# Block-local attention: a group's keys fetched ahead of its queries, with the keys' wait set to their last reader

## The chip, the cores and the metric

The kernel runs on one core of one Trainium2 chip. Its time is device microseconds (us) for one execution, from the first to the last instruction plus what the launch adds around them; the number compared is the median of several executions. One execution was also recorded by the hardware profiler, and all rows below are from it. The engines are PE (TensorE matmul), PEld (its weight loads), DVE (VectorE), ACT (ScalarE), POOL (GpSimd) and SP (SyncE, which in this kernel only issues DMAs, in one queue and in program order).

## The reference, cut to what matters

The program is a two-layer network on x of 8 x 1024 x 128 floats (batch B = 8, T = 1024 tokens, C = 128 channels). The change touches only the first attention:

```python
q, k, v = (layernorm(x) @ W.T split into 16 heads of 8)    # for Wq, Wk, Wv
# tokens in blocks of 64; a block's queries see the block before and their own
scores = q_block @ concat(k_before, k_block).T / sqrt(8)   # 64 x 128 per head
scores = where((j > i) & (j <= i + 64) & not_before_the_first, scores, -1e30)
out    = softmax(scores) @ concat(v_before, v_block)
x      = x + out @ Wo.T
```

Ahead of it stands a gated low-rank expert layer with its normalisation; behind it stand the same layer once more, a quantised product, a latent attention with 8 heads, and the quantised product again.

## The kernel before, in words

The window attention (the stage that the change touches) works in 16 groups: group hb is half hb % 2 of batch hb // 2, so 512 tokens, all 16 heads. A group is 8 steps (HB = 8), one per block of 64 tokens; step n = 8 hb + m. The whole stage is one software pipeline over n, written out by hand. In step n TensorE does, in program order:

- at m = 0 the transposition of the previous group's row maxima (`pe_window_maxima(hb - 1)`, L1013), and only then
- the scores of step n with queries as rows (`pe_window_scores`, its mask product is L1085, its scores L1090). Scores of step n wait for VectorE's maxima of step n - 1, and at m = 0 for the group's queries and keys to have landed (`moved(hb, 0)` and `moved(hb, 1)`, L1079 to L1081);
- the scores of step n - 10 with keys as rows (`pe_window_key_rows`, L1035 and L1042), which count up `key_rows` at 2n + r; at m = 0 they wait for the maxima that SP has moved (L1026);
- the weighing with the values of step n - 12 and later (L1061), the turning back (L1070), and "parts" that a planner placed in two spare banks: among them the projection of group hb's queries and keys ("once", L842), due ten steps ahead of the group.

Queries and keys need a layout that one product can't give: each value split in a high and a low part, and replicated over partitions. So each group goes through memory. ScalarE copies the product's high part into the tile `once` and VectorE the rest (L876, L905); SP writes `once` to `rows_mem` in HBM (`sync_spread`, 8 DMAs for the queries, i = 0, then 8 for the keys, i = 1), and brings it back (`sync_gather`): the queries with 4 DMAs of 256 KB in pieces of 256 bytes (L952), the keys with one DMA of 1 MB in pieces of 2 KB (L948). A gather waits until all of its own writes have landed (`bounced[i]`, L946), and for its place in on-chip memory to be free: the queries' three buffers by L943, the keys' two batches by L945. Both are waits on `key_rows`.

SP's program for the stage (L2135 to L2142) is, for each hb in order: spread queries, spread keys, gather queries, gather keys, and then `sync_move_maxima(hb - 1)` (L971, 4 small DMAs), which waits for the maxima of group hb - 1 to be copied by ScalarE, that is for TensorE to stand at the start of group hb. The next iteration's spread also waits until the gathers of this one have landed (L926). So between the start of group hb - 1 on TensorE and the start of group hb, SP moves the maxima of group hb - 2, spreads group hb and gathers group hb.

Of the kernel before, what the change touches and what calls it, by code (L numbers as in the profile page):

```python
# [27 lines left out]
HB = NB // 2  # L28
# [269 lines left out]
def build_program(nc, x_in, w128, w_mla, w_out_window, w33, w1, consts, out):  # L298
    ctx = ExitStack()
    with ctx:  # L300
# [8 lines left out]
        def signal(name):  # L309
            counts.append(Count(new_sem(name)))  # L310
            return counts[-1]
# [499 lines left out]
        key_rows, exps = signal("window_scores_by_key"), signal("window_exponentials")  # L811
# [110 lines left out]
        def sync_spread(e, hb, i):  # L922


            if hb:
                e.wait_ge(*moved(hb - 1, i))  # L926
            e.wait_ge(*part_act.at(("once", hb, i)))
            e.wait_ge(*part_dve.at(("once", hb, i)))
            for h in range(4):
                rows = slice(h * REP * D0, (h + 1) * REP * D0)  # L930
                into = rows_mem[i, h].rearrange(("(x y) d q c -> y (d q) x c", "(x y) d q c -> x (d q) y c")[i], x=2)
                e.dma_start(into[0], once[rows, i].bitcast(F32)).then_inc(bounced[i], 16)
                e.dma_start(into[1, :, 0], once[rows, i, 0].bitcast(F32)).then_inc(bounced[i], 16)

        def sync_gather(e, hb, i):

            b, half = divmod(hb, 2)
            e.wait_ge(*last_rows_stored)
            if i == 0:
                if hb < QUERY_BUFS:  # L940
                    e.wait_ge(*set_pool.at(("slots", hb)))
                else:
                    e.wait_ge(*key_rows.at(2 * HB * (hb - QUERY_BUFS + 1) - 1))  # L943
            elif b >= 2:
                e.wait_ge(*key_rows.at(2 * HB * (2 * (b - 2) + 2) - 1))  # L945
            e.wait_ge(bounced[i], 128 * (hb + 1))  # L946
            if i:
                e.dma_start(keys[:, b % 2, :, W + half * HALF:W + (half + 1) * HALF].bitcast(F32),  # L948
                            rows_mem[1].rearrange("h p d q c -> (h p d) q c")).then_inc(k_moved[hb % 2], 16)
                return  # L950
            for h in range(4):
                e.dma_start(queries[h * REP * D0:(h + 1) * REP * D0, hb % QUERY_BUFS, :, :, h % 2, :].bitcast(F32).rearrange(  # L952
                    "p q n w -> p (q n) w"),
                    rows_mem[0, h].rearrange("p d q (n w) -> (p d) (q n) w", w=W)).then_inc(q_moved[hb % 2], 16)

        def sync_last_rows(e):


            e.wait_ge(*set_pool.at("last rows"))
            for i in range(2):  # L960
                for h in range(4):
                    e.dma_start(rows_mem[i, h, REP - 1].rearrange("d q c -> (d q) c"),
                                last_rows[:, i, :]).then_inc(last_rows_stored[0], 16)

        def sync_move_maxima(e, hb):

            e.wait_ge(*mx_copied.at(hb))
            for r in range(2):
                for s in range(2):
                    row = (2 * r + s) * REP * D0 + (REP - 1) * D0  # L970
                    e.dma_start(queries[row:row + 1, hb % QUERY_BUFS, :, :, s, :].bitcast(F32).rearrange(  # L971
                        "o q m w -> o (q m) w"),
                        mx_rows[r * QUADS * HB:(r + 1) * QUADS * HB, hb % 2, s * W:(s + 1) * W].bitcast(F32)).then_inc(
                        mx_moved[hb % 2], 16)
# [884 lines left out]
        def sync_move_shift(e, u, i):  # L1859

            e.wait_ge(*shift_steps.at((u, i, 2)))
            queries_free(e, u)
            for t in range(4 * i, 4 * i + 4):
                e.dma_start(q_low[KR:KR + 1, u % Q_BUFS, t * P:(t + 1) * P].bitcast(F32).rearrange(
                    "o (p t) -> o p t", t=1), shift_cols[:, i, t % 4:t % 4 + 1].bitcast(F32)).then_inc(
                    shift_moved[u % Q_BUFS][i], 16)
# [89 lines left out]
        def sync_move_head(e, u):  # L1956

            b, h = divmod(u, NH)
            rows = slice(h % 4 * DC, (h % 4 + 1) * DC)
            if h == 0 and b >= 2:  # L1960
                e.wait_ge(*projected.at((b - 2, 1)))
            e.wait_ge(*o_ready.at(u))
            for q in range(4):
                e.dma_start(o_allT[rows, b % 2, h // 4, q * QUARTER:(q + 1) * QUARTER],
                            o_norm[q * DC:(q + 1) * DC, u % 2, :]).then_inc(o_moved[u % 2], 16)
# [156 lines left out]
        def sync_store(e, b):  # L2122
            e.wait_ge(*x_dve.at(("d", b)))
            e.dma_start(outr[:, b], x[:, b * NT:(b + 1) * NT, :]).then_inc(s_out, 16)

        def sync(e):
            e.dma_start(first_rows[:, :], x_in[:, 0, :]).then_inc(first_landed[0], 16)
            e.dma_start(x[:, 0:NT, :], xr[:, 0]).then_inc(x_landed[0][0], 16)
            e.dma_start(cst[:, :], consts).then_inc(const_landed[0], 16)
            for dst, src in ((Wt, w128), (Wo, w_out_window), (Wt33, w33), (Wt1, w1)):  # L2130
                e.dma_start(dst[:, :], src).then_inc(weights_landed[0], 16)
            for b in range(1, B):
                e.dma_start(x[:, b * NT:(b + 1) * NT, :], xr[:, b]).then_inc(x_landed[b][0], 16)
            sync_last_rows(e)
            for hb in range(2 * B + 1):  # L2135
                if hb < 2 * B:
                    for i in range(2):
                        sync_spread(e, hb, i)
                    for i in range(2):
                        sync_gather(e, hb, i)  # L2140
                if hb:
                    sync_move_maxima(e, hb - 1)  # L2142
            e.wait_ge(*gate_steps.at(("a", "y")))
            for b in range(B):
                e.wait_ge(*x_dve.at(("w out", 2 * b)))
                e.dma_start(first_rows[b:b + 1, :], x[0:1, b * NT, :]).then_inc(first_landed[1], 16)
            e.wait_ge(*x_dve.at(("w", B - 1)))
            e.wait_ge(*weighed.at(units // 4 - 1))
            e.dma_start(Wm[:, :], w_mla).then_inc(mla_landed[0], 16)
            for u in range(B * NH + 2):  # L2150
                if u < B * NH:
                    for i in range(2):
                        sync_move_shift(e, u, i)
                if u >= 2:
                    sync_move_head(e, u - 2)
                b, h = divmod(u, NH)
                if h == 3 and 2 <= b < B:
                    sync_store(e, b - 2)
            sync_store(e, B - 2)
            for half in range(2):  # L2160
                e.wait_ge(*x_dve.at(("d", B - 1, half)))
                ts = slice(half * NT // 2, (half + 1) * NT // 2)
                e.dma_start(outr[:, B - 1, ts], x[:, (B - 1) * NT + half * NT // 2:(B - 1) * NT + (half + 1) * NT // 2, :]
                            ).then_inc(s_out, 16)
            e.wait_ge(s_out, 16 * (B + 1))
# [9 lines left out]
        @block.sync  # L2175
        def _(eng):
            sync(eng)
# [81 lines left out]
```

## Time and profile before

| | us |
|---|---|
| median of 3 runs (lowest to highest) | 1809.43 (1809.35 to 1809.67) |
| the profiled execution, its own time | 1814.3 |
| its span, first to last instruction | 1812.5 |
| PE busy in the span | 1670.4 (92%) |
| DVE busy | 1393.8 (77%) |
| ACT busy | 1137.5 (63%) |
| POOL busy | 1177.3 (65%) |
| window attention, first to last scores of a step (L1085) | 73.6 to 456.2 |
| mean granted TensorE clock, share of full speed | 0.967 |

The page divides the span into 40 slices of 45 us. The DMA engines are busy in the first ten of them (0.4 to 0.6 of their time, 116 to 164 GB/s) and nearly idle from slice 12 on; those ten are the loads, the first expert layer and the window attention. A share is a mean over the 16 DMA engines; packets in flight at the same time on one engine count each, so a short stretch can show slightly more than 1.

### The profile page before, as it was taken

What the parts mean: (1) busy time and instruction counts of PE and PEld (TensorE: products, weight loads), DVE (VectorE), ACT (ScalarE), POOL (GpSimd) and SP (SyncE); (2) the same over time, 40 slices, a digit from 0 to 9 for tenths busy, and PEclk for the clock granted to TensorE, in tenths of its full rate; (3) what the DMA queues carried; (4) which work ended last, traced back from release to release, by engine and by line L of the source; (5) the groups of instructions that cost most, each with busy time, mean ns of one, the idle gap of its engine ahead of it and who ended that gap; (6) DMA issues with size and microseconds to landing.
All of it is one profiled execution on the core that took longest, in us unless ns stands there. A gap on an engine that the chain in (4) does not pass through costs nothing.

```text
span 1812.5 us, 39662 instructions
## 1 busy us (share of the span) xinstructions
PE 1670.4 (92%) x15057; PEld 1223.0 (67%) x15057; DVE 1393.8 (77%) x2976; ACT 1137.5 (63%) x2222; POOL 1177.3 (65%) x909
## 2 busy tenths in 40 slices
PE   4679999999877899999999999999999999999995
PEld 4557777777766567666766766766676677677674
DVE  5557777766597888878888888888887888888862
ACT  5447777777676466666666666666656666665662
POOL 4300111000066498898898988989889898898892
PEclk9889999999887899999999999999999999999997
DMA  4556666654000000000000000001001000100101
GB/s 123 136 140 156 162 156 159 164 136 116 29 1 1 1 10 8 10 8 10 7 13 16 10 8 19 11 7 22 7 10 19 8 10 7 22 7 10 19 10 30
DMA packets 198677, 81.47 MB, mean 45 GB/s; under 512 B 152553, under 2 KB 177493, under 8 KB 198357
## 3 DMA queue, kind: packets, MB, share of 16 engines
q1 hardware_dynamic: 198484, 78.93, 19.5%
q8 instruction: 119, 1.95, 0.5%
q14 instruction: 74, 0.60, 0.1%
HBM read 39.79 MB, written 29.88 MB: 38 GB/s over the span
## 4 chain that ended last, share of the span: by engine, by line
PE 54%; DVE 11%; POOL 2%; issue 1%; ACT 1%; DMA 0%; SPq 0%; POOLq 0%; ACTq 0%
PE pair L1825 12%; PE pair L1878 11%; PE pair L1882 11%; PE pair L1936 10%; DVE amax L1833 4%; PE pair L1929 4%; PE pair L1650 2%; DVE o_inv L1946 1%; PE pair L1641 1%; DVE stats L485 1%; POOL w_mix L1907 1%; PE pair L1664 1%; DVE q_low L1754 1%; DVE cq L1765 1%; DVE key_hl L1768 1%
## 5 line engine op out<-in xcount | busy, mean ns | idle before, releaser
L1893 ACT ACTIVATE prob<-pair 128x512 f32<-128x512 f32 x1024 | 604.4, 597 | 422.2 <-PE pair L1882 359.6
L1833 DVE TENSOR_REDUCE amax<-pair 128x1 f32<-128x512 f32 x1024 | 670.3, 682 | 133.9 <-PE pair L1825 131.8
L1825 PE MATMUL pair<-key_hl,q_hi 128*128 128x512 f32 x1024 | 437.8, 430 | 11.2 <-DVE amax L1833 7.1
L1878 PE MATMUL pair<-q_hi,key_hl 128*128 128x512 f32 x1024 | 405.2, 396 | 2.6 <-ACT prob L1893 2.6
L1882 PE MATMUL pair<-q_low,key_h 65*128 65x512 f32 x1024 | 406.0, 396 | 0.0
L1907 POOL TENSOR_TENSOR w_mix<-w_mix,prob 128x1024 f32<-128x1024 f32 x160 | 382.3, 2389 | 25.2 <-ACT prob L1893 8.5
L1907 POOL TENSOR_TENSOR Wm<-Wm,prob 128x1024 f32<-128x1024 f32 x155 | 369.6, 2384 | 20.8 <-ACT prob L1893 4.1
L520 POOL TENSOR_SCALAR veps<-mv 128x8 f32<-128x8 f32 x47 | 11.4, 243 | 452.6 <-DVE mv L493 451.2
L1825 PEld LDWEIGHTS pair<-key_hl,q_hi 128*128 128x128 f32 x1024 | 196.1, 192 | 115.9 <-issue 51.0
L1936 PE MATMUL pair<-prob,values 128*32 128x256 f32 x4096 | 247.2, 382 | 0.0
L1186 DVE TENSOR_REDUCE mx_neg<-pair 128x4 f32<-128x512 f32 x256 | 164.9, 687 | 94.8 <-PE pair L1090 94.1
L1878 PEld LDWEIGHTS pair<-q_hi,key_hl 128*128 128x128 f32 x1024 | 195.5, 191 | 44.3 <-ACT prob L1893 9.4
L1882 PEld LDWEIGHTS pair<-q_low,key_h 65*128 65x128 f32 x1024 | 192.5, 188 | 44.6
L1936 PEld LDWEIGHTS pair<-prob,values 128*32 128x32 f32 x4096 | 127.5, 110 | 100.9 <-issue 25.0
L1136 ACT ACTIVATE yT<-pair 128x512 f32<-128x512 f32 x256 | 138.6, 593 | 72.3 <-PE pair L1042 70.3
L1946 DVE RECIPROCAL o_inv<-pair 128x256 f32<-128x256 f32 x64 | 112.5, 1758 | 59.8 <-PE pair L1929 59.8
L542 ACT ACTIVATE y<-x,mean_neg,rstd 128x128 f32<-128x128 f32 x336 | 137.7, 485 | 19.0 <-POOL mean_neg L528 18.9
L1090 PE MATMUL pair<-keys,queries 64*128 64x128 f32 x1024 | 100.5, 317 | 0.0
L1042 PE MATMUL pair<-queries,keys 64*128 64x128 f32 x1024 | 97.0, 309 | 0.0
L1702 ACT ACTIVATE q_hi<-pair 128x512 fp32r<-128x512 f32 x128 | 75.7, 591 | 20.0 <-PE pair L1641 20.0
L1754 DVE TENSOR_TENSOR q_low<-pair,q_hi 64x512 fp32r<-64x512 f32 x128 | 86.3, 675 | 2.2 <-ACT q_hi L1702 2.2
L1090 PEld LDWEIGHTS pair<-keys,queries 64*128 64x128 f32 x1024 | 82.7, 199 | 3.7
(209 smaller groups left out, 2232.8 us busy)
## 6 DMA issues: line engine op xcount, KB each, us to landing
rows_mem<-once SPq DMA_DIRECT2D x128, 128.0 KB, 2.0
queries<-rows_mem SPq DMA_DIRECT2D x64, 256.0 KB, 4.5
keys<-rows_mem SPq DMA_DIRECT2D x16, 1024.0 KB, 7.1
rows_mem<-once SPq DMA_DIRECT2D x128, 64.0 KB, 1.9
q_low<-shift_cols SPq DMA_DIRECT2D x512, 0.5 KB, 2.0
yT<-o_norm SPq DMA_DIRECT2D x256, 32.0 KB, 1.9
x<-x_dram SPq DMA_DIRECT2D x8, 512.0 KB, 7.3
out_dram<-x SPq DMA_DIRECT2D x7, 512.0 KB, 3.4
```

The lines of the kernel that those rows point to most:

```text
L542: ins = e.activation(y_of(stage, b)[:, t, :], x[:, b * NT + t, :], ACT.Identity, bias=mean_neg[:, k, t:t + 1], scale=rstd[:, k, t:t + 1])
L1090: ins = e.matmul(bank(S_BANKS[r])[:, q * P:(q + 1) * P], queries[rows, hb % QUERY_BUFS, q, m].rearrange("p s w -> p (s w)"), keys[rows, b ...
L1136: e.activation(pT[:, u % P_TURNED].rearrange("p q k -> p (q k)"), key_row_bank(*divmod(u, 2)), ACT.Exp).then_inc(*exps.up(u))
L1186: e.tensor_reduce(mx_neg[:, hb % 2, r, :, m], bank(S_BANKS[r]).rearrange("p (q k) -> p q k", q=QUADS), AX_X, ALU.max, negate=True).then_in ...
L1825: e.matmul(row_bank(("row", r, i)), q_hi[:, k, t * P:(t + 1) * P], key_hl[:, b % 2, i * HALF:(i + 1) * HALF], start=True, stop=True, skip_ ...
L1833: e.tensor_reduce(amax1[:, u % 2, t, i:i + 1], row_bank(("row", r, i)), AX_X, ALU.max).then_inc(*row_maxed.up((r, i)))
L1878: e.matmul(bank(j), key_hl[:, b % 2, ks], q_hi[:, k, sl], start=True, stop=False, skip_group_check=True)
L1882: e.matmul(bank(j), key_h1[:, b % 2, ks], q_low[:, k, sl], start=False, stop=True, skip_group_check=True).then_inc(*key_scored.up((g, half)))
L1893: e.activation(prob1[:, g % P_BUFS, half * HALF:(half + 1) * HALF], bank(K_BANKS[(2 * g + half) % 3]), ACT.Exp, scale=SCALE1).then_inc(*ke ...
L1907: e.tensor_tensor(into, into, p, ALU.add).then_inc(*summed_keys.up(g))
L1936: ins = e.matmul(bank(PVB)[q * DC:(q + 1) * DC, 0:QUARTER], values[:, b % 2, t, :], prob1[:, g % P_BUFS, q * QUARTER:(q + 1) * QUARTER], s ...
L1946: e.reciprocal(o_inv[:, u % 2, :], row_bank(("total", u, 0))[:, 0:QUARTER]).then_inc(*o_inverse.up(u))
```

## The change

Two edits in the SP program. The gathers of a group are issued in the order keys, queries where it was queries, keys; and the keys' wait for their place names the last step that reads it, in place of the last step of the batch:

```diff
             elif b >= 2:
-                e.wait_ge(*key_rows.at(2 * HB * (2 * (b - 2) + 2) - 1))
+
+                e.wait_ge(*key_rows.at(2 * (HB * (hb - 4) + (HB if half == 0 else HB - 1)) + 1))
             e.wait_ge(bounced[i], 128 * (hb + 1))
...
                     for i in range(2):
                         sync_spread(e, hb, i)
-                    for i in range(2):
+                    for i in (1, 0):
                         sync_gather(e, hb, i)
```

With b = hb // 2, the old value is the last step of group 2 (b - 2) + 1: for half 0 (hb = 2b) that is step 8 (hb - 2) - 1. The new value is step 8 (hb - 3) for half 0, seven steps earlier, since the first step of the second half also reads the last block of the first half. For half 1 the new value is step 8 (hb - 3) - 1; the old one is the same step, as hb = 2b + 1. Nothing else differs: the same DMAs, with the same sizes and the same semaphores.

## Rows read from the trace of the kernel before

**Rows 1.** The page's busy times: engine, us, share of the span, instructions.

```profile
PE 1670.4 (92%) x15057; PEld 1223.0 (67%) x15057; DVE 1393.8 (77%) x2976; ACT 1137.5 (63%) x2222; POOL 1177.3 (65%) x909
```

**Rows 2.** Waits in 60 to 480 us: who for whom, sum us, times, longest.

```profile
PE pair L1085 <- DMA keys<-rows_mem: 16.9, 9, 4.2
```

**Rows 3.** PE in order of time: start, us; in brackets the idle time before.

```profile
313.39 0.27 PE L1013 MATMUL pair<-cst,mx_neg 128*64 128x128 f32 x1
315.34 0.39 PE L1085 MATMUL pair<-mask_bf,both_rows 64*128 64x512 bf16 x2 [1.68 <-DMA keys<-rows_mem]
...
364.06 0.61 PE L1085 MATMUL pair<-mask_bf,both_rows 64*128 64x512 bf16 x2 [2.73 <-DMA keys<-rows_mem]
...
413.99 0.39 PE L1085 MATMUL pair<-mask_bf,both_rows 64*128 64x512 bf16 x2 [0.74 <-DMA keys<-rows_mem]
```

**Rows 4.** SP's queue around group 10, in order of time: start, us, line.

```profile
303.22 0.42 SPq L933 DMA_DIRECT2D rows_mem<-once  x1
303.75 3.76 SPq L952 DMA_DIRECT2D queries<-rows_mem  x4
307.63 0.78 SPq L948 DMA_DIRECT2D keys<-rows_mem  x1
314.37 2.46 SPq L971 DMA_DIRECT2D queries<-mx_rows  x4
316.94 0.51 SPq L932 DMA_DIRECT2D rows_mem<-once  x1
```

**Rows 5.** DMAs issued in 303.2 to 308.5: KB each, median us to landing.

```profile
rows_mem<-once SPq DMA_DIRECT2D x1, 64.0 KB, 1.9
...
queries<-rows_mem SPq DMA_DIRECT2D x4, 256.0 KB, 4.8
keys<-rows_mem SPq DMA_DIRECT2D x1, 1024.0 KB, 7.6
```

**Rows 6.** Windows around group 10; last three: TensorE clock, DMA share, GB/s.

```profile
305.00:306.00 1.00, 1.00 (x19) 0.90 (x16) 0.61 (x1) 0.90 (x4) 0.00 (x0) 1.00 0.62 144
306.00:307.00 1.00, 1.00 (x10) 1.00 (x11) 0.96 (x4) 0.98 (x2) 0.00 (x0) 1.00 1.08 245
...
312.00:313.00 1.00, 1.00 (x8) 0.73 (x7) 0.98 (x3) 0.86 (x2) 0.00 (x0) 1.00 1.01 375
313.00:314.00 1.00, 0.66 (x3) 0.07 (x1) 0.94 (x7) 0.64 (x2) 0.00 (x0) 1.00 0.29 107
314.00:315.00 1.00, 0.00 (x0) 0.00 (x0) 0.97 (x6) 0.34 (x2) 0.54 (x2) 1.00 0.09 35
```

**Rows 7.** SP's queue ahead of group 12.

```profile
351.49 0.43 SPq L933 DMA_DIRECT2D rows_mem<-once  x1
352.02 3.77 SPq L952 DMA_DIRECT2D queries<-rows_mem  x4
```

**Rows 8.** The last spread write of group 12, issued 351.49: us to landing.

```profile
rows_mem<-once SPq DMA_DIRECT2D x1, 64.0 KB, 3.6
```

**Rows 9.** Windows of group 9, and of groups 10 and 12 from first scores.

```profile
291.30:313.40 22.10, 21.66 (x331) 17.50 (x329) 17.09 (x40) 16.05 (x35) 0.00 (x0) 1.00 0.67 167
...
315.30:339.00 23.70, 22.61 (x337) 18.46 (x337) 16.65 (x46) 18.73 (x43) 3.88 (x7) 1.00 0.65 159
364.10:390.80 26.70, 25.66 (x337) 20.57 (x337) 16.75 (x46) 18.89 (x43) 2.82 (x6) 0.88 0.56 140
...
363.90:370.70 6.80, 6.64 (x68) 5.27 (x70) 1.59 (x3) 2.76 (x7) 0.58 (x3) 0.50 0.50 121
```

**Rows 10.** SP's gather ahead of group 9, an odd group.

```profile
281.93 2.13 SPq L948 DMA_DIRECT2D keys<-rows_mem  x1
```

**Rows 11.** The DMA of Rows 10: KB, us to landing.

```profile
keys<-rows_mem SPq DMA_DIRECT2D x1, 1024.0 KB, 7.0
```

**Rows 12.** PE at the start of group 9.

```profile
291.52 0.39 PE L1085 MATMUL pair<-mask_bf,both_rows 64*128 64x512 bf16 x2
```

**Rows 13.** SP's own waits in 120 to 480 us: sum us, times, longest.

```profile
SPq L971 <- ACT mx_rows L1104: 110.1, 14, 19.2
SPq L928 <- DVE once L905: 14.6, 6, 7.0
```

## The prediction, made before the change was run

> **What bounds the kernel now.** I read the busy times first: PE is busy 92% of the span, far above the other engines [rows 1], so what matters is where PE stands still. The table of waits, cut to the window attention, has one large entry besides PE's give and take with VectorE: the first product of a group waits for the keys' DMA, 16.9 us in 9 waits, the longest 4.2 us [rows 2]. In order of time these waits stand before the first scores of groups 1, 2, 4, 6, 8, 10, 12, 14 and 15; three of the nine are shown, with 1.68, 2.73 and 0.74 us [rows 3]. Next comes SP's queue. Ahead of group 10 it issues the last write of the spread at 303.22, the queries' four gathers from 303.75 (3.76 us for the four), the keys' one at 307.63, and then nothing until the maxima at 314.37 [rows 4]. The keys land 7.6 us after their issue, at 315.2 [rows 5], and the scores start at 315.34 [rows 3]. So an even group starts when its gather has landed. SP's path sets that: maxima moved, 16 writes, 5 reads, landing. An odd group is different: group 9's keys are issued at 281.93 and land 7.0 us later, 288.9 [rows 10, 11], and its scores begin at 291.52 [rows 12], 2.6 us of slack, because the even group before it has taken longer on PE.
>
> The DMA engines' share of busy time completes the picture. The first gather packets show at about 305, 1.3 us after the first issue; from 306 to 313 the share is about 1 (245 GB/s with the queries' small pieces, 375 GB/s with the keys' large ones), and then falls to 0.29 and 0.09 while one or two engines finish [rows 6]. The gather is bound by the DMA engines, not by SP's issuing.
>
> **The wait edit.** For even groups the keys' place is free seven steps sooner, for odd ones the value is the same. For this to be worth anything SP must stand at that wait today. It doesn't: before group 10 the write at 303.22 ends at 303.64, the queries' gather starts at 303.75 and the keys' starts 0.12 us behind it [rows 4], and SP's waits in the stage are for the maxima and for the projection, none for the keys' or queries' place [rows 13]. Besides, the queries' gather of an even group needs the same old value, and a group starts only when both have landed. I cost this edit at nothing, from either side. What it does is make the other edit possible without a stall ahead of the keys.
>
> **The order edit.** The same five DMAs with the same bytes; what moves is which wait is in front. The keys' gather needs the keys' writes in memory, and those are issued last. Today SP covers their landing with the queries' issues: the last write lands at 303.22 + 1.9 = 305.1 [rows 4, 5], and the keys' issue at 307.63 finds that long done. With the keys first, SP stands until 305.1, with the queries' four gathers queued behind it although their own writes landed long before. The keys issue at 305.1 and not the queries at 303.75: everything starts 305.1 - 303.75 = 1.35 us later. PE waits for both kinds, so bringing the keys early gains nothing by itself. The backlog is the same 2 MB on the same engines, so it ends 1.35 us later, unless the end becomes cheaper. There is a reason for a little of that: from 313.2, where the bulk is through, the keys take until 315.2 to land [rows 5, 6]; the last query piece is a quarter of the size and may have a shorter tail. I take 0.25 us off: 1.1 us for a group like this one. Groups 1, 2, 8 and 10 are such.
>
> Groups 4, 6, 12 and 14 have a late write. Before group 12 the last write is issued at 351.49 and lands 3.6 us later, at 355.1 [rows 7, 8]; the queries' first gather is issued at 352.02, so the new start is 3.1 us later. Less than that can be lost, as most engines are idle while one finishes the writes, and today's gather can't pass that engine's backlog either. Its end would stand about 1.3 us (the start-up seen in rows 6) behind the landing of the write in place of directly behind it. The bounds are 0 and 3.1 us; I take 1.5, nearest to the start-up time.
>
> Which groups does it cost? The gather of group hb is released by the maxima of group hb - 2, moved when PE enters group hb - 1, before that group's own wait for keys. So in an even group the added delay adds to its wait one for one; in an odd group it eats slack that the even group's longer wait has just given back, so it costs nothing. Of the two neighbours 14 and 15 that both wait, the second's added delay is covered by the first's by the same rule; 1 and 2 both pay, as group 2's gather waits for a projection behind group 1. That is eight groups: 4 x 1.1 + 4 x 1.5 = 10.4 us. Bounds: 0 below, where the tail gives all back, and 4 x 1.35 + 4 x 3.1 = 17.8 above.
>
> SP's later work has room: the queries' last issue would end at about 305.1 + 0.8 + 3.8 = 309.7 against 314.37 for the maxima, and the next spread, which now also waits for the queries' landing at about 316.5, begins at 316.94 today [rows 4]. If the landing came later than that, the 2.6 us of slack of the odd group behind it would cover it [rows 11, 12].
>
> **The clock.** Group 12 waits 2.73 us, and then the granted clock is 0.50 (1.2 GHz) from 363.9 to 370.7; from its first scores on, the group takes 26.7 us where group 10, after a wait of 1.68 us and with the clock at 1.00 throughout, takes 23.7 [rows 3, 9]. So an idle time of 2.73 us has cost another 3.0 us, and 1.68 us has not. With the new delays the waits of groups 4, 6, 8, 10 and 14 go from 0.74 to 1.68 us up to about 2.2 to 3.0 us, right between these two rows or just above them. Bounds: no further fall, or all five, 15 us. I take two, 6.0 us.
>
> **The sum** is 10.4 + 6.0 = 16.4 us. It is made in one profiled execution of 1814.3 us (span 1812.5), 4.9 us above the median of the runs; as a difference of 0.9% it carries over to the median: 1809.4 + 16.4 = 1825.8 us. The later stages are bound by their own engines and shift as a whole.
>
> **The rivals.** First, no change: the tail gives back what the start loses. For it: 2.0 us lie between the end of the bulk and the keys' landing, more than 1.35. Against it: part of this is an engine that is behind in total work, and order does not help that one. The price is a few tenths in each of 8 groups either way: 1808 to 1812, and no fall of the clock.
>
> Second, faster: what counts is how fast the last DMA lands after its issue. A piece of 256 KB lands in 4.8 us, one of 1 MB in 7.6 [rows 5]. Keys issued at 305.1, queries from 306.0, the last of the four at about 309.0, landing 4.8 us later: 313.8, where the keys land at 315.2 today. If that holds, the wait of 1.68 us is gone, as PE's transposition stands at 313.39; over all groups most of the 16.9 us [rows 2] would go, say 10, and with it the 3.0 of the clock in group 12: 1796 to 1800. It decides where SP's issuing, not the DMA engines, sets the end, that is where the share in the gather is clearly under 1. Against it, the share is at 1 for seven microseconds [rows 6], and the queries would then stand behind 1 MB of keys. The Trainium skill would side with this rival: DMA: Bandwidth & Descriptors, section Anatomy of one DMA, gives about 2.0 us plus bytes over 436 GB/s for one transfer, an estimate of 4.4 us for the keys alone; no row here shows that rate, the best second of a gather shows 375 GB/s and the queries' 245.
>
> Third, the same mechanism but dearer: every late write costs its full 3.1 us and the clock falls in all five further groups, 17.8 + 15 = 33 us, 1842.
>
> Fourth, the change doesn't reach what it names: were the keys' place the binding wait somewhere, the earlier value would gain. Nothing of the kind is among SP's waits [rows 13]; its chance is in that of the second.
>
> **How the numbers follow.** My forecast has 0.73, no change 0.12, faster 0.08, the dear one 0.07. The range leaves out the faster case, about half of no change and most of the dear one: 1811 to 1836. A measurement of this kernel tells about 0.2% (3.6 us) from no change. Slower by more than that: 0.80, faster: 0.08, within: 0.12; the forecast's own low end, with a small loss per group and no fall of the clock, is still over 4 us.
>
> **What would show it.** Right: SP issues the keys' gather first, about 1.9 us behind the last write and with nothing between; the queries land last, and PE's wait at L1085 is now put down to the queries' DMA, with about 27 us in place of 16.9; odd groups 3 to 13 start without a wait; stretches at clock 0.50 follow some even groups' starts. Wrong: PE's waits at L1085 get shorter, the share of the DMA engines is under 1 in the gather, or the queries land less than 12.0 us behind the last write's issue (303.22 to 315.2 today), as a group would then start no later than now.

## The result, and the profile after

The changed kernel takes 1828.1 us (median; 1827.5 to 1832.7) against 1809.6 us before (1809.4 to 1811.4): 18.6 us more, a ratio of 1.0103 with a 95% interval of 1.0083 to 1.0123. The forecast was 1825.8 us.

The page of the profiled execution after (1832.7 us, span 1830.9) has the same work on each engine, to be held against [rows 1]:

```profile
PE 1673.7 (91%) x15057; PEld 1222.9 (67%) x15057; DVE 1394.1 (76%) x2976; ACT 1138.5 (62%) x2222; POOL 1177.5 (64%) x909
```

So PE is busy for 3.3 us more (1673.7 against 1670.4) and idle for 15.1 us more, 18.4 us of span in all. Source lines behind the changed wait have moved by one: L1086 is the first product of a group, L953 the queries' gather, L949 the keys'. The table of waits of the kernel after, in 60 to 480 us (sum, times, longest), against [rows 2]:

```profile
PE pair L1086 <- DMA queries<-rows_mem: 30.5, 12, 6.3
```

PE now waits for the queries, as they land last, and for 30.5 us in place of 16.9. In order of time at groups 6, 8, 10, 12 and 14 (start, us; idle time in brackets), against [rows 3]:

```profile
226.79 0.39 PE L1086 MATMUL pair<-mask_bf,both_rows 64*128 64x512 bf16 x2 [3.71 <-DMA queries<-rows_mem]
277.95 0.39 PE L1086 MATMUL pair<-mask_bf,both_rows 64*128 64x512 bf16 x2 [3.58 <-DMA queries<-rows_mem]
327.70 0.39 PE L1086 MATMUL pair<-mask_bf,both_rows 64*128 64x512 bf16 x2 [2.18 <-DMA queries<-rows_mem]
377.53 0.61 PE L1086 MATMUL pair<-mask_bf,both_rows 64*128 64x512 bf16 x2 [2.29 <-DMA queries<-rows_mem]
431.07 0.39 PE L1086 MATMUL pair<-mask_bf,both_rows 64*128 64x512 bf16 x2 [4.07 <-DMA queries<-rows_mem]
```

A single group misleads: group 12 waits 2.29 us where it waited 2.73 before, and group 10 2.18 where it waited 1.68. What counts is the sum over the groups.

SP's queue ahead of group 10 after, against [rows 4] (start, us, line):

```profile
315.02 0.43 SPq L933 DMA_DIRECT2D rows_mem<-once  x1
316.96 0.59 SPq L949 DMA_DIRECT2D keys<-rows_mem  x1
317.68 6.79 SPq L953 DMA_DIRECT2D queries<-rows_mem  x4
326.23 2.43 SPq L972 DMA_DIRECT2D queries<-mx_rows  x4
```

The landings of those DMAs, against [rows 5] (KB each, median us from issue):

```profile
keys<-rows_mem SPq DMA_DIRECT2D x1, 1024.0 KB, 5.6
queries<-rows_mem SPq DMA_DIRECT2D x4, 256.0 KB, 7.1
```

The hole is where it was expected: the last write is issued at 315.02 and the keys' gather 1.94 us later, where before the queries' gather came 0.53 us behind the last write. SP's own waits in 120 to 480 us have a new line, against [rows 13]:

```profile
SPq L972 <- ACT mx_rows L1105: 65.9, 14, 19.9
SPq L928 <- DVE once L905: 26.7, 6, 5.0
SPq L947 <- DMA rows_mem<-once: 23.8, 13, 3.3
SPq L932 <- DMA queries<-rows_mem: 1.3, 2, 0.9
```

SP stands for the landing of the keys' writes in all 13 groups of the stretch, 1.8 us each. The DMA engines' share over the same gather (last three columns: TensorE clock, share, GB/s), against [rows 6]:

```profile
317.00:318.00 1.00, 1.00 (x16) 0.90 (x15) 0.75 (x2) 0.90 (x4) 0.00 (x0) 1.00 0.00 0
318.00:319.00 1.00, 1.00 (x11) 1.00 (x10) 0.97 (x3) 0.97 (x2) 0.00 (x0) 1.00 0.62 45
319.00:320.00 1.00, 1.00 (x11) 1.00 (x10) 0.95 (x5) 0.00 (x0) 0.00 (x0) 1.00 0.84 305
320.00:321.00 1.00, 1.00 (x16) 0.84 (x15) 0.78 (x3) 0.67 (x2) 0.00 (x0) 1.00 1.04 408
...
325.00:326.00 1.00, 0.52 (x2) 0.00 (x0) 0.95 (x10) 0.64 (x3) 0.00 (x0) 1.00 0.80 177
326.00:327.00 1.00, 0.00 (x0) 0.00 (x0) 0.84 (x4) 0.20 (x2) 0.68 (x2) 1.00 0.73 163
```

The DMA engines move nothing for a microsecond behind the keys' issue and 45 GB/s in the next. That the keys start more slowly than the queries did is true only in part, as finer windows show. First the kernel after, whose keys are issued at 316.96:

```profile
318.20:318.40 0.20, 0.20 (x5) 0.20 (x3) 0.20 (x1) 0.20 (x2) 0.00 (x0) 1.00 0.83 61
...
319.20:319.40 0.20, 0.20 (x5) 0.20 (x4) 0.17 (x2) 0.00 (x0) 0.00 (x0) 1.00 0.72 246
```

Then the kernel before, whose queries are issued at 303.75:

```profile
305.00:305.20 0.20, 0.20 (x10) 0.20 (x7) 0.00 (x0) 0.19 (x2) 0.00 (x0) 1.00 0.09 23
...
305.60:305.80 0.20, 0.20 (x8) 0.20 (x6) 0.20 (x1) 0.19 (x2) 0.00 (x0) 1.00 1.01 230
```

The first packets show about 1.3 us behind the issue in both. The window with over 200 GB/s begins 2.2 us behind it with the keys in front and 1.9 us with the queries in front. At the end the share falls slowly, at 163 to 177 GB/s, and the scores start 0.7 us after the last busy window.

Last the clock. Both kernels run at half speed for about 17 us in the first two groups (from 83 to 102 us). The stretches of the stage behind that, after the change (clock 0.50 in each; first column PE busy):

```profile
121.30:131.50 10.20, 6.12 (x66) 4.74 (x68) 1.29 (x2) 2.71 (x7) 1.44 (x3) 0.50 0.72 142
227.10:230.50 3.40, 3.40 (x52) 2.86 (x48) 1.29 (x2) 1.09 (x2) 0.00 (x0) 0.50 0.75 180
278.30:281.70 3.40, 3.40 (x52) 2.78 (x48) 1.29 (x2) 1.09 (x2) 0.00 (x0) 0.50 0.73 176
329.50:332.90 3.40, 3.40 (x42) 2.45 (x31) 0.72 (x2) 2.42 (x7) 0.00 (x0) 0.50 0.57 137
377.30:384.10 6.80, 6.57 (x68) 5.11 (x70) 1.52 (x3) 2.76 (x7) 1.09 (x3) 0.50 0.52 122
431.90:435.30 3.40, 3.40 (x46) 2.26 (x45) 1.28 (x2) 1.60 (x3) 0.00 (x0) 0.50 0.66 158
```

That is 26.3 us of PE's busy time at half speed, behind the waits of groups 2, 6, 8, 10, 12 and 14. Before it was 12.3 us behind the first two groups, in two stretches: the one of group 12 [rows 9] and this one behind the 4.2 us wait of group 2:

```profile
121.60:128.40 6.80, 5.68 (x62) 4.38 (x62) 1.29 (x2) 2.29 (x6) 0.57 (x3) 0.50 0.54 128
```

Waits and clock together make the difference. The window stage, from its first to its last scores, grew by 19.1 us (73.6 to 456.2 before, 73.6 to 475.3 after), the whole span by 18.4, so all the other stages together differ by 0.7 us. Of the 19.1, 13.6 are the waits at the groups' starts (30.5 - 16.9), and 14.0 us more of busy time at half speed, at 1.6 us for each 3.4 us (measured below), are 6.6. The sum of 20.2 is 1.1 too large, and the 6.6 in it is an estimate.

### The profile page after: what moved, and what is told of

It reads as the page before. It is cut to its first block, busy times and chain, and to the rows that moved or that the text cites. A ratio compares the mean times of both kernels' runs of the same rounds, so it can differ in the third digit from the quotient of the medians.

```text
span 1830.9 us, 39662 instructions
## 1 busy us (share of the span) xinstructions
PE 1673.7 (91%) x15057; PEld 1222.9 (67%) x15057; DVE 1394.1 (76%) x2976; ACT 1138.5 (62%) x2222; POOL 1177.5 (64%) x909
## 4 chain that ended last, share of the span: by engine, by line
PE 53%; DVE 10%; POOL 2%; issue 1%; ACT 1%; DMA 0%; SPq 0%; POOLq 0%; ACTq 0%
PE pair L1826 12%; PE pair L1879 10%; PE pair L1883 10%; PE pair L1937 10%; DVE amax L1834 4%; PE pair L1930 4%; PE pair L1651 2%; DVE o_inv L1947 1%; PE pair L1642 1%; DVE stats L485 1%; POOL w_mix L1908 1%; PE pair L1665 1%; DVE q_low L1755 1%; DVE key_hl L1769 1%; DVE cq L1766 1%
## 5 line engine op out<-in xcount | busy, mean ns | idle before, releaser
L1086 PE MATMUL pair<-mask_bf,both_rows 64*128 64x512 bf16 x256 | 52.1, 404 | 47.0 <-DMA queries<-rows_mem 30.5
```

## The experiments

Each was timed beside the kernel before on its own chip, whose median was 1810.6 to 1812.6 us with single runs from 1804 to 1821. So the ratios are to be compared, not microseconds across calls.

### Each edit alone

```diff
# order alone: the old value of the wait, and
-                    for i in range(2):
+                    for i in (1, 0):
                         sync_gather(e, hb, i)
# wait alone: the new value, and for i in range(2) kept
```

Expected of the order alone:

> Only the order of the two gathers is changed (keys, then queries); the keys' wait for their place keeps its old value. Theory (the order alone makes the loss, since the place has been free for some microseconds when the writes land): as the whole change, 1824 to 1832 us. Rival (with the keys in front their old wait, seven steps later for even groups, would now hold SP, and the new value is what avoids this): slower than the whole change by several us, 1833 or more, with SP standing at the key scores' semaphore.

Expected of the wait alone:

> Only the keys' wait is set to their last reader; the order stays queries, keys. Theory: no instruction ever stood at this wait, so the time is that of before, 1809 to 1811 us, with PE's waits at the first scores of a group at 16.9 us in sum. Rival (the place was a hidden limit): faster by over 3 us, under 1806.

Measured: order alone 1832.4 us, ratio 1.0115 (1.0067 to 1.0163); wait alone 1811.8 us, ratio 1.0011 (0.9986 to 1.0036). The order makes the whole loss. The wait's value is worth nothing that can be told from the noise in either order: the ratio with the order alone is that of the whole change (1.0103) within its interval. SP has no wait for the keys' place in its profile, so the rival's cause isn't there. PE's waits for the gather are 32.9 us, where the whole change has 30.5:

```profile
PE pair L1085 <- DMA queries<-rows_mem: 32.9, 12, 6.7
```

### The exposed landing alone

```diff
             if i == 0:
+                e.wait_ge(bounced[1], 128 * (hb + 1))    # queries gather: the keys' writes too
                 ...
             e.wait_ge(bounced[i], 128 * (hb + 1))
```

> The kernel before, in its old order, with one wait more: the queries' gather also waits until the keys' writes have landed. This puts the one exposed landing in without the new order. Theory A (the loss is the exposed landing and nothing else): 1824 to 1830 us, as the whole change. Theory B (the landing costs 1.35 us a group, and the keys in front cost again as much, because their first data come 2.0 us behind the issue against 1.3 for a quarter of the queries, and because the queries' landing then closes the gather): about half, 1815 to 1821 us.

Measured: 1832.1 us, ratio 1.0107 (1.0074 to 1.0140). Five of its six runs are at 1831.9 to 1833.5 us, so one added wait, with the DMAs in their old order, costs as much as the whole change. Theory A holds by the time. The sixth run, at 1817.7 us, is the one that was profiled, so the trace shows the mild form. There SP's queue is as expected (last write 309.90, queries 2.05 us behind it, keys last), and the table of waits, shown below it, has PE at 24.0 us, midway between 16.9 and 30.5:

```profile
309.90 0.62 SPq L933 DMA_DIRECT2D rows_mem<-once  x1
311.95 4.47 SPq L954 DMA_DIRECT2D queries<-rows_mem  x4
316.53 0.73 SPq L950 DMA_DIRECT2D keys<-rows_mem  x1
```

```profile
PE pair L1087 <- DMA keys<-rows_mem: 24.0, 12, 6.7
```

Two things make this execution milder than the profiled one of the whole change, and the length of SP's path is not one of them (the table in the part on the prediction). No last write is late: each lands in 1.9 to 2.1 us, where after the change three took 3.5 to 3.7. And behind group 2 the clock falls twice, for 3.4 us each, where it fell five times. What the other five executions did in those 14 us no trace shows; the section on the hardware has a candidate.

### Keys ahead of queries without the exposed landing

First the spread alone was turned, then the projection too:

```diff
                     for i in (1, 0):              # both kernels
                         sync_spread(e, hb, i)
                     for i in (1, 0):
                         sync_gather(e, hb, i)
...
-            first += [("once", after, i) for i in range(2)]    # the second kernel only
+            first += [("once", after, i) for i in (1, 0)]
```

Spread turned:

> The whole change, and the spread also writes the keys first and the queries second. The keys' gather then finds its own writes landed and goes out right behind the last write; its 0.6 us of issue and its start-up lie beside the landing of the queries' writes. Theory A (exposed landing): most of the loss comes back, 1808 to 1813 us. Theory B (start-up and issue behind a 1 MB transfer also count): part comes back, 1814 to 1820 us. Rival (ordering of the data itself is what costs): no change against 1828.

Measured: 1885.4 us, ratio 1.0406 (1.0369 to 1.0443). Outside all three expectations, for a reason that none had: the keys' projection comes behind the queries' in the pipeline, and SP, in order, now stood for it with everything else behind. SP's waits in 120 to 530 us:

```profile
SPq L928 <- DVE once L905: 121.3, 13, 11.0
SPq L947 <- DMA rows_mem<-once: 14.1, 14, 2.8
```

This run tells nothing of the theories. The second kernel takes this wait away.

> The whole change with keys ahead of queries all the way: projection, spread and gather. The run before this one (keys spread first, but projected second) stood at the keys' projection, whose rest VectorE takes two steps behind the queries'. Here the first spread again finds its projection ready, and the keys' gather goes out right behind the last write, so no landing is exposed ahead of the first gather. Theory A (the exposed landing of the last write carries the loss): 1806 to 1814 us. Rival (keys ahead of queries in the gather cost by themselves): stays at 1822 or more.

Measured: 1811.0 us, ratio 0.9990 (0.9977 to 1.0002). The keys still go ahead of the queries in the gather, but their issue stands 0.54 us behind the last write (SP's queue, first), and PE's waits are back at 18.3 us (table of waits, second):

```profile
304.51 0.43 SPq L933 DMA_DIRECT2D rows_mem<-once  x1
305.05 0.59 SPq L949 DMA_DIRECT2D keys<-rows_mem  x1
306.47 6.37 SPq L953 DMA_DIRECT2D queries<-rows_mem  x4
```

```profile
PE pair L1086 <- DMA queries<-rows_mem: 18.3, 9, 5.2
```

So both directions agree: put the exposed landing in without the order and the loss is there, take it out with the order kept and the loss is gone. The order of the data as such costs nothing.

### The clock

Extra transpositions in front of the wait for a group's data, so that PE has less idle time there; they change no value.

```diff
             if m == 0:
+                for _ in range(FILL.get(hb, 0)):
+                    e.transpose(bank(S_BANKS[0])[:, 0:P], eye, eye)
                 e.wait_ge(*moved(hb, 0))
# after, first: FILL = {2: 24, 6: 16, 8: 16, 10: 12, 12: 12, 14: 16}
# after, more:  FILL = {4: 30, 6: 30, 8: 30, 10: 30, 12: 30, 14: 30}
# before:       FILL = {2: 24, 12: 14}
```

> The whole change, and 12 to 24 extra transpositions on TensorE (about 0.13 us each, of the constant unit matrix into a scores' bank that is overwritten next) in front of the wait for the group's queries at groups 2, 6, 8, 10, 12 and 14, so that the waits there are mostly filled with work. Nothing of the result changes. Theory (part of the loss is the clock at 0.50 after these waits, about 17 us more of it than before, worth some 8 us): 1818 to 1822 us, and no stretch at 0.50 between 130 and 470 us. Rival (the clock's stretches cost nothing because SP's path sets the groups' starts): 1827 to 1831 us.

Measured: 1831.3 us, ratio 1.0098 (1.0082 to 1.0113). Outside the theory's range, but not an answer: the clock fell all the same, as in this stretch behind group 6:

```profile
228.60:253.70 25.10, 24.05 (x336) 19.20 (x337) 16.60 (x46) 18.83 (x43) 2.37 (x4) 0.93 0.64 149
...
229.90:233.30 3.40, 3.40 (x44) 2.26 (x44) 0.81 (x2) 2.43 (x6) 0.00 (x0) 0.51 0.83 198
```

With 30 transpositions:

> The whole change with 30 extra transpositions (about 0.11 us each, 3.3 us, as the run with fewer of them showed) ahead of the wait at groups 4, 6, 8, 10, 12 and 14, where the waits are 2.2 to 4.1 us. With 12 to 16 of them 1.8 to 2.4 us stayed idle and the clock fell all the same; now under 1 us stays idle. Theory (the falls are a cost on top of the waits, 1.6 us for each 3.4 us at half speed): no stretch at 0.50 between 135 and 450 us, 1820 to 1824 us. Rival (a fall costs nothing because the group's start is set by SP anyway): 1827 to 1833 us.

Measured: 1826.4 us, ratio 1.0083 (1.0055 to 1.0110). The clock is at 1.00 from 135 to 450 us, and group 6's work takes 23.6 us from its first scores, where after the change, without filling and with one stretch of 3.4 us at half speed, it took 25.2:

```profile
229.00:252.60 23.60, 22.55 (x337) 18.37 (x337) 16.63 (x46) 18.68 (x43) 2.45 (x5) 1.00 0.61 152
...
135.00:450.00 315.00, 300.93 (x4411) 247.28 (x4410) 219.57 (x568) 228.53 (x512) 25.97 (x44) 1.00 0.64 152
```

The same stretch of the kernel after:

```profile
226.80:252.00 25.20, 24.15 (x336) 19.52 (x337) 16.61 (x46) 18.74 (x43) 2.36 (x4) 0.93 0.62 147
```

That is the price of 1.6 us used above, and it is free of the wait itself. Groups 8 and 10 give it again: from their first scores to the next group's it is 23.8 us here and 25.4 us after the change. Read by stage, the profiles bear it out: from group 4's first scores to the last scores of the stage it is 298.96 us after the change (176.35 to 475.31) and 290.22 us here (179.54 to 469.76). That is 8.7 us less, for 20.2 us of busy time at half speed that are gone, which the price puts at 9.5. These are two single executions. The whole kernel gains less than theory said. In this execution group 4 began 2.5 us later, counted from the stage's start. And the fixed 3.44 us of filling is longer than the wait in some groups: at group 8 the DMA engines are quiet from 276.8, and the filling runs until 279.4. Between the theory's 1820 to 1824 and the rival's 1827 or more, the time decides nothing by itself, and its interval overlaps that of the change. Shown are the price per stretch and, in one pair of executions, its sum over a part of the stage; the clock's share of the whole, 6.6 us, is worked out from it.

> The kernel before, with 24 such transpositions ahead of group 2 and 14 ahead of group 12, the two waits after which its clock fell in the profile. Theory: 3 us for group 12 and up to 3 for group 2, so 3 to 6 us faster than before. Rival: no difference.

Measured: 1810.9 us, ratio 0.9997 (0.9989 to 1.0006). No difference, as the rival had it. In its profile the fall at group 12 is gone, the one at group 2 lasts 3.4 us in place of 6.8, and a new one of 3.4 us stands at 410.6, behind group 14's wait. Filling two waits took away one fall and did not keep a new one from coming elsewhere.

### Shortening SP's path

If SP's path from one group's start to the landing of the next group's data sets the starts, then taking something off it must help the kernel before. The four DMAs of the maxima stand in it.

```diff
-                if hb:                               # SP's program
-                    sync_move_maxima(e, hb - 1)
...
         def pool_window(e):
             for n, items in enumerate(plan_w):
+                if n % HB == 0 and 0 <= n - HB < PAIRS:
+                    sync_move_maxima(e, n // HB - 1)
```

> The kernel before, in the old order, with the four small DMAs of the maxima issued by GpSimd, which is nearly idle in this stage, in place of SP. SP's path from one group's start to the landing of the next group's keys loses 2.5 us of issue and its tie to TensorE's group start. Theory (SP's path sets the starts of even groups): waits at the first scores fall from 16.9 us to under 6, the clock stays at 1.00 behind them, 1790 to 1800 us. Rival (the DMA engines' throughput sets the landing): the keys land no earlier and the time is that of before, within 3 us.

Measured: 1807.1 us, ratio 0.9970 (0.9960 to 0.9981). Faster by about 5 us and short of the 10 to 20 expected. PE's waits in 60 to 480 us:

```profile
PE pair L1086 <- DMA keys<-rows_mem: 9.5, 6, 5.8
PE pair L1036 <- DMA queries<-mx_rows: 5.6, 8, 1.1
```

The keys' waits fell from 16.9 to 9.5 us, 7.5 of them at groups 1 and 2. But the maxima, issued behind GpSimd's normalisation work at even groups, now come late, and PE waits 5.6 us for them. ScalarE in GpSimd's place, and GpSimd with its other work one step back:

```diff
# ScalarE: behind its copy of the maxima
+                    sync_move_maxima(e, hb)
# GpSimd, maxima first
-                    if n == window_norm_start(b) + 3:
+                    if n == window_norm_start(b) + 4:
                         norm_pool(e, "w", b, True)
```

> The kernel before, with the maxima's four DMAs issued by ScalarE right behind its own copy of the maxima. SP's path is as short as with GpSimd, the maxima start 0.9 us behind the group and not up to 3.6, but ScalarE stands about 2.4 us for the issues. Theory (the shorter path of SP is what counts): 1802 to 1808 us. Rival (ScalarE's exponentials are late by the issues and TensorE waits for them, about 1 to 2 us in each of 15 groups): 1815 to 1830 us.

Measured: 1826.1 us, ratio 1.0089 (1.0062 to 1.0117). The rival's cause and size: ScalarE is late with its exponentials, and TensorE waits for them at the key scores, 19.1 us where before it was 4.5:

```profile
PE pair L1036 <- ACT yT L1138: 19.1, 20, 2.2
```

> As the run with the maxima on GpSimd, with GpSimd's normalisation work (2.6 us ahead of every even group) moved one step back, behind the maxima's DMAs. Theory (the maxima's late issue made the 0.6 to 1.1 us waits at the key scores of groups 3, 5, 7, 9 and 11): these go, about 4 us, 1802 to 1804 us. Rival (the normalisation, now late, holds ScalarE instead): 1806 to 1812 us.

Measured: 1803.4 us, ratio 0.9958 (0.9941 to 0.9974), faster than both kernels and inside the theory's range. The waits for the maxima are down from 5.6 to 2.0 us:

```profile
PE pair L1086 <- DMA keys<-rows_mem: 10.3, 5, 4.3
PE pair L1036 <- DMA queries<-mx_rows: 2.0, 3, 1.2
```

Last the kernel with the keys first everywhere, and the maxima's DMAs on GpSimd in the first form, with the normalisation work in its old place:

> Keys ahead of queries in projection, spread and gather, and the maxima's DMAs issued by GpSimd. The first alone gave the time of before, the second 5 us less. Theory (two savings on the same path of SP): 1800 to 1806 us. Rival (what is left of the waits is in groups 1 and 2 and in the maxima's own landing, which neither touches): 1805 to 1809 us, as the second alone.

Measured: 1806.0 us, ratio 0.9978 (0.9963 to 0.9992). In the theory's range and in the rival's; by its ratio it is GpSimd's edit alone (0.9970), so bringing the keys first adds nothing even where it costs nothing.

## Why the prediction was right, point by point

- **What bounds the stage.** Right: SP's path sets the starts of even groups. A lengthened path lost 1.1%, a shortened one gained 0.4%, with the same products on TensorE.
- **The wait edit at nothing.** Right, from both sides: 1.0011 with it alone, 1.0115 without it and with the order.
- **The order edit: 10.4 us, 1.1 us a group from the exposed landing.** Right in its mechanism, shown in both directions, and right in the size for one group. The path from the issue of the last write to a group's first scores can be read in every profile. The table has the five groups (1, 2, 8, 10 and 15) that wait for the gather in all five kernels and whose last write lands in 1.9 us:

| us from last write to first scores | 1 | 2 | 8 | 10 | 15 | mean |
|---|---|---|---|---|---|---|
| before | 10.92 | 10.67 | 11.55 | 12.12 | 11.67 | 11.39 |
| keys first everywhere (no exposed landing) | 11.04 | 11.02 | 11.47 | 11.46 | 11.72 | 11.34 |
| old order, one wait more (landing exposed) | 12.34 | 12.51 | 12.91 | 12.68 | 12.45 | 12.58 |
| the whole change | 12.20 | 12.35 | 13.07 | 12.68 | 12.62 | 12.58 |
| order alone | 12.31 | 12.72 | 13.12 | 12.97 | 12.83 | 12.79 |

The exposed landing adds 1.2 us, the same with the queries in front as with the keys in front (1.4 with the order alone). So nothing of it is the keys' slower start or the queries' landing last, and the 1.35 us of later start less the 0.25 us taken off came out; but the reason given for the 0.25, a shorter tail of the queries, isn't it, as the old order has the same 1.2. In sum the forecast was low, 10.4 us against 13.6 us of waits, with errors on both sides. Groups 1, 2, 8 and 10 wait 6.0 us longer in place of 4.4, as a group's wait also depends on when PE comes to it. Groups 4, 6, 12 and 14 wait 4.8 us longer in place of 6.0, and the odd groups 3, 5, 13 and 15 wait 2.7 us longer in place of nothing.
- **Late writes, 1.5 us each.** The groups and the size were both wrong, in opposite directions. After the change the late writes are those of groups 3, 6 and 14 (landing after 3.7, 3.6 and 3.5 us), not of 4 and 12, which wait 1.01 and 2.29 us, less than before. Where a write is late the path is 14.9 us, where the four groups with a late write before had 12.0: 2.9 us more, near the bound of 3.1 and not 1.5. The reading behind the 1.5 was that today's gather can't pass the late write. The trace before shows that it does. At group 12 the last write lands at 355.1, and in this window ahead of that the engines move 112 KB, where the late write has 64 KB and nothing but the gather is issued behind it:

```profile
354.00:354.40 0.40, 0.40 (x6) 0.40 (x4) 0.40 (x2) 0.40 (x2) 0.00 (x0) 1.00 1.26 280
```

- **Odd groups cost nothing.** Right for 7, 9 and 11. Groups 3, 5 and 13 wait 1.12, 0.68 and 0.24 us, and group 15 waits 1.91 us where it waited 1.23. The slack that was said to cover them had been read off group 9 alone, and group 3 also had a late write.
- **The clock, 6.0 us.** The sum is right by luck. The forecast was two further falls at 3.0 us each. There were four (groups 6, 8, 10 and 14), each 3.4 us long in place of the 6.8 us of group 12's, at 1.6 us each. Twice the number at half the price gives 6.4, and 6.6 with what group 2's stretch grew.
- **The rivals.** No change, by a tail that gives all back: the tail didn't. Faster, because a short transfer lands last: behind the 1 MB a piece of 256 KB lands in 7.1 us (median of the four) and not in 4.8, and the four issues themselves take 6.79 us and not 3.8, so the gather did not end earlier. The 4.4 us that the prediction estimates for the keys alone from the Trainium skill (DMA: Bandwidth & Descriptors, section Anatomy of one DMA) isn't met either: issued in front of all else, the keys of group 10 land in 5.6 us; and the page gives that fit for DMAs issued by GpSimd, where SP issues these. The dear case: the clock fell in four of its five groups, at about half its price, and its full delay of 3.1 us per late write nearly came true, but in two even groups and not in four.

## What to carry to other kernels

In a queue that works in order, a wait is priced by what could have gone out in its place: of two loads that both need a round trip through memory, issue first the one whose writes went out first, so that its issue covers the landing of the other's. Before moving a load forward, look which of two waits ends last at the reader: when both are needed together, the earlier landing of one is worth nothing. And when a queue's path from one stage's start to the next stage's data sets the pace, move small transfers that aren't needed by it to an idle engine's queue, in front of that engine's other work.

## What the runs showed of the hardware

- Some falls of the clock come at even distances. After the change three begin at 227.1, 278.3 and 329.5, 51.2 us apart, and groups 6 and 8 start 51.2 us apart too (226.8 and 278.0), while group 10 starts 49.8 us later and the next two falls are 47.8 and 54.6 us apart; in the first filled kernel they are at 178.7, 229.9, 281.1, 332.3 and 383.5, again 51.2 apart, and the filling changed neither the spacing nor the time. With the clock held up, groups 8, 10 and 12 start 49.2 us apart. This would give a kernel two steady times, as the one with the exposed landing alone has (1817.7 and 1832 us); that this is the cause was not shown.
- One idle time doesn't tell whether the clock falls: 1.80 us of idle behind 1.8 us of transpositions was followed by a fall, 1.68 us in the kernel before [rows 3] was not, and neither was 2.53 us at group 6 of the kernel before with filling elsewhere.
- The four issues of the queries took SP 6.79 us behind the 1 MB transfer (6.37 in the keys-first kernel), against 3.76 in front of it [rows 4]. It cost the path nothing in the keys-first kernel (11.34 us against 11.39 before). That the queue in front of the DMA engines was full would explain the long issues and wasn't tested. Whether SP or the DMA engines then set the last landing stays open too: their share is 0.80 and 0.73 in its last two busy microseconds.
